# Summing the columns of the second halves on GpSimd in the pooling and mixing stages

## The reference

```
x = x + _L0_conv_ref(_gn(x), ...)   # 8x8 patches, each convolved 3x3 by the expert that its mean picks, gated
x = x + _L1_conv_ref(_gn(x), ...)   # pooled mean -> sigmoid routing -> mixed 3x3 weights, convolution
x = x + _L2_conv_ref(_gn(x), ...)   # nearest of 512 code words at each pixel
x = x + _L3_conv_ref(_gn(x), ...)   # deformable 3x3: bilinear samples at 9 predicted points, then 9 taps
```

## Time and profile before

| | us |
|---|---|
| median of three timed runs | 1838.69 |
| lowest and highest | 1831.52, 1839.75 |
| the profiled execution | 1828.76 |
| span of its trace | 1827.0 |
| busy: TensorE, VectorE | 1572.8, 1527.7 |
| busy: GpSimd, ScalarE | 1203.4, 1105.7 |

### The profile page before, as it was taken

The page is one execution under the profiler, slowest core; times in us unless marked ns, Lnnn a source line. Parts: engine busy times, 40 slices in busy tenths (PEclk is TensorE's granted clock), DMA queues, the critical chain, the costliest instruction groups (busy, mean ns, idle before and its releaser), DMA issues.

```text
span 1827.0 us, 42287 instructions
## 1 busy us (share of the span) xinstructions
PE 1572.8 (86%) x15584; PEld 1289.7 (71%) x15584; DVE 1527.7 (84%) x3113; ACT 1105.7 (61%) x1547; POOL 1203.4 (66%) x1403
## 2 busy tenths in 40 slices
PE   4686389889898999989898998989899899988998
PEld 3644376689666885678666896668866797668997
DVE  5467389989898888989898898988989788988998
ACT  2011366568554775567665676548755677658985
POOL 2043277786677666786677766776677856778764
PEclk9788699999999999999998999999999999999999
DMA  6536875699657976589656986579765895336552
GB/s 138 130 95 161 185 221 163 169 231 227 189 162 195 237 205 181 172 216 224 191 159 169 246 212 200 155 193 242 210 186 159 218 216 157 85 88 171 160 154 70
DMA packets 284244, 326.12 MB, mean 179 GB/s; under 512 B 209444, under 2 KB 223780, under 8 KB 280192
## 3 DMA queue, kind: packets, MB, share of 16 engines
q1 hardware_dynamic: 240712, 228.88, 47.7%
q0 software_dynamic: 35856, 80.87, 17.8%
q10 hardware_dynamic: 7472, 13.67, 2.4%
HBM read 253.50 MB, written 56.40 MB: 170 GB/s over the span
## 4 chain that ended last, share of the span: by engine, by line
PE 43%; DVE 16%; DMA 9%; DVEq 8%; POOL 8%; issue 7%; SPq 5%; ACT 2%; ACTq 1%; POOLq 0%
PE bank L1362 26%; DMA words<-in_codebook,code 5%; PE bank L1490 4%; DVE code L1229 4%; DVEq L1228 4%; POOL fetched L638 3%; PE bank L1444 3%; POOL words L661 3%; DVEq L1023 3%; PE bank L1473 3%; PE bank L1342 2%; DVE samp L1024 2%; SPq L469 2%; DVE weighted L1014 2%; PE bank L1349 2%
## 5 line engine op out<-in xcount | busy, mean ns | idle before, releaser
L638 POOL DMA_INDIRECT fetched<-row_pairs,corner x768 | 742.3, 967 | 378.8 <-issue 201.8
L1362 PE MATMUL bank<-lent,tent 128*128 128x160 f32 x6144 | 941.4, 308 | 5.3 <-issue 4.4
L1362 PEld LDWEIGHTS bank<-lent,tent 128*128 128x128 f32 x6144 | 871.6, 195 | 98.1 <-issue 60.1
L770 ACT ACTIVATE tent<-lent,row_at_sb 128x768 f32<-128x768 f32 x512 | 448.8, 924 | 50.3 <-PE bank L1362 44.9
L774 ACT ACTIVATE tent<-tent 128x1536 f32<-128x1536 f32 x256 | 380.0, 1484 | 20.6
L1006 DVE TENSOR_TENSOR strip<-bank,near 128x480 f32<-128x480 f32 x512 | 331.0, 648 | 43.6 <-PE bank L1362 39.2
L661 POOL DMA_INDIRECT words<-in_codebook,code x256 | 244.8, 956 | 103.6 <-issue 53.1
L1024 DVE TENSOR_REDUCE samp<-strip 128x96 f32<-128x480 f32 x414 | 270.4, 653 | 37.0 <-issue 1.3
L1490 PE MATMUL bank<-cb,xs 64*128 64x512 f32 x512 | 218.1, 658 | 30.1 <-DVE code L1229 15.8
L851 ACT COPY xs<-xn 32x128 f32<-32x128 f32 x256 | 75.5, 295 | 230.9 <-PE bank L1490 213.0
L759 ACT COPY samp_t<-bank 96x384 f32<-96x384 f32 x256 | 119.8, 468 | 152.6 <-PE bank L1349 65.1
(11 more groups left out here) (152 smaller groups left out, 1356.8 us busy)
## 6 DMA issues: line engine op xcount, KB each, us to landing
lent<-z_rows SPq DMA_DIRECT2D x256, 384.0 KB
picked_weights<-arena SPq DMA_DIRECT2D x14, 1800.0 KB
arena<-picked_weights SPq DMA_DIRECT2D x21, 720.0 KB
arena<-windows SPq DMA_DIRECT2D x276, 50.0 KB, 2.0
arena<-xp SPq DMA_DIRECT2D x96, 136.0 KB
fetched<-row_pairs,corner POOLq DMA_INDIRECT x768
arena<-row_pairs SPq DMA_DIRECT2D x64, 160.0 KB
slice<-picked_weights SPq DMA_DIRECT2D x14, 720.0 KB
```

What stands on the lines that cost most here:

```text
L638: pool.indirect_dma_start(fetched[:, N % FETCHES, k].rearrange("p q c -> p (q c)"), None, pairs_dram[b % 2], bass.IndirectOffsetOnAxis(ap= ...
L770: act.activation(w[:, piece], zs[:, N % SPREADS, :], ACT.Abs, bias=row_at[:, piece:piece + 1])
L1362: m = pe.matmul(STRIPS[j % 3][:, XW * C * e:XW * C * (e + 1)], tent[:, N % TENTS, c, DENSE * d + e], picture[:, b % 2, i, c], start=(c == ...
```

## The change

The table `ON_POOL` gets the second halves in two stages. Nothing else is changed, and all the code that the table reaches is in the kernel already:

```diff
-        ON_POOL = {"features": (0,), "pool": (0,), "mix": (0,), "conv1": (0,), "norm2": (0,)}
+        ON_POOL = {"features": (0,), "pool": (0, 1), "mix": (0, 1), "conv1": (0,), "norm2": (0,)}
```

## The result

The change made the kernel slower. No measurable change had been forecast. The profiled execution of the change took 1849.45 us, above its median as the one of before lay under its own, so the two traces differ by 20.7 us, twice what the medians do. I read from them where the time went, and from the medians how much.

What follows compares the result with a forecast made beforehand. Bound: the chain into TensorE's second convolution, which waits for mixed weights and stacked rows, either possibly later. Copies allow 0.3 us in five groups, other terms cost nothing: 1838.69 - 1.5 = 1837.2 us, range 1825 to 1845.

Steps and rivals of the forecast that it cites:

- VectorE's gain ahead of the mixing: Sums of halves 13 and 15 leave VectorE, 0.75 us each: mixed weights 1.5 us earlier per group, 10.5 us at most.
- the company of the two engines: GpSimd's additions beside VectorE's mixing instructions slow these: 0.7 us a group taken, bounds 0 and 1.7.
- The copies: Stacked-row copies ahead of the second convolution don't move and are late next, limiting the gain to 1.5 us in all.
- The 0.3 us in five groups: Convolution start earlier by 0.3 us in each group where the mixing had ended its wait; 1.5 us in all.
- GpSimd: GpSimd's queue through the mixing stage: about a microsecond late, caught up before the score stage; cost nothing.
- the slower rival: GpSimd late into the score stage, at the gather of 703.37: 13.3 us more, 1850.5 us; chance 0.09.
- TensorE's new wait: TensorE's transposes of halves 12 and 13 wait 0.9 us for GpSimd's sum, then continue as before; cost nothing.
- the clock rival: TensorE's shorter pause ahead of the convolution keeps its clock up in five groups: 10 us less, 1828.7; chance 0.09.
- the opposite case: Convolution passes of groups 6 and 7 lose the upper clock level: 3.4 us more.
- the GpSimd rival: Delays of GpSimd's three sums exceed 5.8 us idle time and reach the score stage: 13.3 us more; chance 0.09.

Runs made afterwards that it cites:

- the change with ten fillers: The change plus ten useless unit-matrix products on TensorE ahead of the convolution's wait in groups 1 to 7: 1824.67 us against 1834.16 before, ratio 0.9951.
- the held half: The change, no useless products, with TensorE's strips of half 17 also waiting for VectorE's first four mixing instructions: 1832.83 us against 1834.16 before, ratio 0.9981.

## Why the prediction was wrong

*VectorE's gain ahead of the mixing* was right as far as L1171: 0.73 us after the strip for 0.75. The 1.5 us up to the end of the mixing didn't arrive. I had taken 0.7 us of it for the company of the two engines, with 1.7 as the bound. In group 3, L1173, L1189 and L1191 lost 0.45 + 0.43 + 0.93 and L1181 won 0.35: 1.5 us. The 0.45, L1173 beside a gather, had been no term of the sum. In the mean of the seven groups the mixing ended 10.41 us after the first copy's issue, and 10.43 before. The rule of the Trainium skill that was cited (GPSIMD Engine Reference, section Key points) is borne out: L1191, with two SBUF inputs, went from 0.309 us to 0.377 in the mean.

*The copies* were named rightly as what is late next. The 0.3 us in five groups was mis-sized: the convolution starts 10.92 us after the first copy and started 10.74 before, as the copies themselves came later: the twelve issues took 7.77 us in the mean for 7.67, with one or two longer than the usual 0.59 us in each of the seven groups (0.80 and 0.69 in group 3) and in three of the seven before. In this pair of traces, in place of 1.5 us won, 7 x 0.18 = 1.3 us were lost. Why issues take longer stays open.

*GpSimd* was in time for the score stage, as forecast, and the slower rival that I had kept did not occur. Half 13's sum, though, did not come as late as forecast.

*TensorE's new wait* is the step that failed. "The wait moves, the end of it does not. Cost nothing": I had half 13's sum arrive on GpSimd about 0.9 us after TensorE would ask for it, and so the strips of half 17 at their old time. Counted from the first copy of group 3, the sum was forecast for 681.6 - 676.58 = 5.0 us and came at 680.13 - 675.66 = 4.47; TensorE was forecast for 680.7 - 676.58 = 4.1 and came at 680.27 - 675.66 = 4.61, as the longer L1173 had taken 0.45 of its 0.75 us. So no wait was left, and in six of seven groups the sum came in time. The strips came earlier (680.93 - 675.66 = 5.27 us after the first copy, 682.15 - 676.58 = 5.57 before), the convolution started later (10.97 for 10.41), and the pause between them grew by 0.3 + 0.56 us, from 3.04 to 3.91.

This pause was the very thing I had in the clock rival, with the wrong sign: "becomes shorter by the gain and by the later transposes". Both halves of that sentence were drawn from terms that did not hold, and the price of the opposite case, 3.4 us for the two groups at the upper clock, left out that a stretch can fall further than the 9.8 us of most: to 12.4 and more, at 0.62 to 0.64. That the median, 1844.76, still lies between 1825 and 1845 is luck: the upper end was set by the price of the GpSimd rival, which did not occur.

The size: 17.4 us in the one pair of traces, 10.6 in the medians. The granted clock of every run's whole span bears it out beyond the traces: its median is 0.9425 in the 22 runs of the change and 0.946 to 0.947 in the 93 runs of the kernel before on three chips, 0.948 without half 13's sum and 0.952 in the change with ten fillers; and within the change 1832.76 us had 0.952, 1855.34 had 0.940. Worked out from these, the difference of 0.004 is an estimated 0.004 x 1845 = 7 us of TensorE's time at the upper level. That the clock behind the pause carries the loss is shown by the fillers and, more weakly, by the held half, which leave all the sums in place and take the loss away.

That half 13's sum sets it off is shown in the traces by the strips' earlier end, in the times less firmly, as its own interval reaches to no change. Why a pause of some 3.7 us ended in 12.5 us in most groups of the change, but in 9.8 in its last, and one of 3.3 in 8.0 or 12.5, stays open.

The Trainium skill (TensorE: Matmul & The Clock Gate, section Part 1) says that the throttled clock is the default and that activity releases it. The traces agree: with ten useless products ahead of the convolution the granted clock was 1.00 in all seven stretches of the change, and in six of seven of the kernel before.

## What to carry to other kernels

Before an instruction is moved off the path, ask which engine it lets run ahead, and what that engine waits for next: if the end of that wait is fixed by a transfer, the gain is spent as a longer pause. If this engine is TensorE, the pause has a price of its own, which shows as the granted clock of the stretch behind it; a few products in the pause, sized from their trace so that they end before the wait does, or the same work done later, buy it back. Work moved between VectorE and GpSimd should be priced with which instructions then stand beside each other, additions and gathers alike: here twice 0.75 us were won on VectorE and 1.5 lost.

## What the runs showed that was not expected

- Adding work made the kernel faster: ten useless products, 2.4 us together, in each of seven groups, 0.4% off the kernel before and 1% off the change.
- The clock stays down after a pause for a good part of the work that follows, in group 3 of the change: 5.35 us for a pass of 2.78, then 3.57 for strips of 1.90, and only the second pass at 2.78 again.
- Company slows more than two-input instructions, and a gather can be the company. L1173, one input of 128 x 16, went from 0.23 to 0.68 us in group 3. In six of the seven groups of the change it took 0.66 us or more, beside a gather (L638) and not beside an addition, and ended within 0.02 us of it. Before, it lay beside a gather in three groups and took 0.23 us in all, so company alone does not decide it.
